# A gated attention and FFN block: the head laid anew, and the row statistics put between the low halves of the RELU

## The chip, the cores and the metric

One core of a Trainium2 chip runs the whole program. The metric is the device time in microseconds of one execution; the engines are PE (TensorE, matmul), DVE (VectorE), ACT (ScalarE), POOL (GpSimd) and SP (SyncE, which here only issues DMAs).

## What is computed

```python
# x: (8, 512, 256); all W of the attention 256x256; W1: (1024, 256), W2: (256, 1024)
xn = layernorm(x)                                  # no weight, no bias
q, k, v = (gelu(xn @ W1 + b1) @ W2 + b2 for each of q, k, v)     # gelu exact
scores = tril(q @ k.T) / sqrt(256 * 512)           # masked by zeros, no softmax
s = layernorm(scores @ v) * ln_w + ln_b
Wq = clip(round(W / (mean(abs(W)) + 1e-5)), -1, 1) # for W1 and W2 of the FFN
g = silu(relu(xn @ Wq1.T + b1) @ Wq2.T + b2)
out = x + s * g
```

## The kernel before

The kernel goes through the eight batches one after the other; each is a block of 512 rows of 256 channels. `batch(0, first=True)` is written out, batches 1 to 6 run in a hardware loop (on DVE and POOL batch 6 is written out), batch 7 is written out. Each engine has its own instruction stream in the order of the code, and semaphores (`wait_ge`, `then_inc`) join the streams. No scheduler moves anything.

To keep fp32 accuracy each operand is held as a high half (rounded, made by ACT or POOL) and a low half (source minus high half, made by DVE), and a product is three products: hi·hi, lo·hi and hi·lo (`split_product`, L771, whose inner matmul is L777). A batch goes, on PE, through these stages: layer one (six products of 512 columns, in PSUM banks 0 to 5, each followed by two GELUs on ACT and a low half `g_lo` on DVE), K (two products, banks 6 and 7), V (two banks), F1 (eight products against the quantised W1, each followed by two RELUs on ACT, L436 and L437, and a low half `r_lo` on DVE, L664), D and S (the scores), Y0 and Y1 (the FFN's second layer, which needs all eight `r_lo` and the quantised W2), O (scores times V) and Y2. A bank is claimed (`claim`, L748) by waiting for whoever reads its last content.

The statistics of x are made two batches ahead: `x_statistics(i + 2)`, L504, runs four `bn_stats` (L511) and `aggregate` (six small instructions, L490) on DVE, between `y_bias` and `o_scale(0)`. POOL takes the power for `x_rstd`, SP writes mean and rstd to DRAM and reads them back broadcast; POOL then normalises the transposed x.

Batch 0 has to do more. The *head* is what stands before it: DVE makes the statistics of x of batch 0 and normalises it in two halves (`x_normalise0`, L523), PE runs nine warm-up matmuls on constants (`WARM_UP`, L769) after POOL has made all five constants (`consts_made`, the last of them `causal`, L257), then `fold_biases` (six one-column products), then eight transposes of `xn` (L762), which ACT copies to `xT_hi` (L406) and DVE splits. Inside batch 0's layer one PE also folds W2q with W2k into one weight (`fold_weights`, FOLD in banks 6 and 7). The quantisation of W1 and W2 needs the sum of absolute values: of W1 by DVE (L613, after the second `g_lo`), of W2 by ACT (`abs_sum2`, after the last GELU); PE adds over partitions (`sum_partitions`, L799, into GAMMA in bank 3), DVE makes the threshold and compares (`quantise1` in two halves, `quantise2` for five eighths of W2), POOL compares the rest of W2 (`quantise_rest`, L300, after both halves of W1). `quantise2` stands behind all eight `r_lo` of batch 0, and PE's Y0 waits for it (`w2_quantized`, L883).

SP issues the loads in the order x(0) first half, W2q, W1k, W2k, W1q, x(1), W1v, W2v, W1 (raw1, 1 MB), W2 (raw2, 1 MB). ACT issues the other half of x(0), the bias columns, and later all four rows of `rows` broadcast to 128 partitions (L403, 512 KB).

## Time and profile before

| what | value |
|---|---|
| median of 3 runs | 320.83 us (319.23 to 322.04) |
| the profiled execution | 320.46 us |
| span of its trace | 318.7 us |
| PE busy | 307.7 us (97%) |
| DVE busy | 246.6 us (77%) |
| ACT busy | 220.1 us (69%) |
| POOL busy | 136.5 us (43%) |
| DMA | 19.06 MB, mean 60 GB/s |
| the chain that ended last | PE 49%, DVE 17%, ACT 15%, issue 15%, POOL 2% |

The span runs from the first to the last instruction on the core; the device time has 1.8 us more around it. Busy time of PE counts overlapping matmuls as one, so 97% says that PE nearly always had a matmul under way, and not that each ran at its best rate. The chain is read back from the last instruction to whatever released it. Line numbers are those of the kernel before.

### The profile page before, as it was taken

Reading aid. Unit: us, or ns where it says so; the run is one execution under the profiler, and the core shown is the slowest. Engines: PE = TensorE matmul, PEld = TensorE weight load, DVE = VectorE, ACT = ScalarE, POOL = GpSimd, SP = SyncE. Lnnn points to the kernel's source line nnn. Section 1 sums busy time; section 2 is a strip of 40 time slices with the busy share of each in tenths; the row PEclk is TensorE's granted clock in tenths of the full one; section 3 lists DMA queues with packets and bytes.
Section 4 is the critical chain, followed back from the end, with each engine's and each line's share of the span. In section 5 each row is a group of like instructions: output and inputs, shape, how many; then the busy total and the mean of one; then the engine's idle time right before and its main releaser. Section 6 shows DMA issues by size and latency. Waiting matters only on the chain.

```text
span 318.7 us, 5664 instructions
## 1 busy us (share of the span) xinstructions
PE 307.7 (97%) x1850; PEld 273.7 (86%) x1850; DVE 246.6 (77%) x544; ACT 220.1 (69%) x416; POOL 136.5 (43%) x105
## 2 busy tenths in 40 slices
PE   7899979999999999999999999999999999999994
PEld 7788879888997899888997889978998889988894
DVE  4589797965979669795879759796697958696687
ACT  3386936959487667858579494886678585794862
POOL 3691733349052570609334390526706093322200
PEclk9999999999999999999999999999999999999999
DMA  7950014520004100050003300041000500010001
GB/s 234 386 172 2 0 68 140 182 76 0 3 1 132 66 0 0 31 167 0 0 0 98 100 0 0 0 135 63 0 0 32 166 0 0 0 66 3 0 3 66
DMA packets 15212, 19.06 MB, mean 60 GB/s; under 512 B 1760, under 2 KB 12512, under 8 KB 15200
## 3 DMA queue, kind: packets, MB, share of 16 engines
q1 hardware_dynamic: 14496, 17.98, 17.1%
q10 hardware_dynamic: 704, 0.93, 0.8%
q8 instruction: 6, 0.10, 0.1%
q14 instruction: 6, 0.05, 0.1%
HBM read 14.69 MB, written 4.22 MB: 59 GB/s over the span
## 4 chain that ended last, share of the span: by engine, by line
PE 49%; DVE 17%; ACT 15%; issue 15%; POOL 2%; DVEq 1%; ACTq 0%; POOLq 0%
PE bank L777 47%; ACT r_hi L436 6%; ACT bank L437 5%; DVE gw L686 2%; DVE gw L701 2%; DVE e L675 2%; DVE x_stats L511 2%; DVE s L652 1%; PE bank L769 1%; DVE g_lo L593 1%; DVE s L649 1%; DVE e L608 1%; POOL o_rstd L343 1%; ACT s_hi L444 1%; DVE s_lo L659 1%
## 5 line engine op out<-in xcount | busy, mean ns | idle before, releaser
L664 DVE TENSOR_TENSOR r_lo<-bank,r_hi 128x512 fp32r<-128x512 f32 x64 | 44.1, 691 | 35.1 <-ACT bank L437 35.1
L436 ACT ACTIVATE r_hi<-bank,col 128x512 fp32r<-128x512 f32 x64 | 46.9, 733 | 24.5 <-PE bank L777 24.5
L437 ACT ACTIVATE bank<-bank,col 128x512 f32<-128x512 f32 x64 | 45.3, 709 | 0.0
L314 POOL TENSOR_TENSOR y<-y,xn 128x512 f32<-128x512 f32 x12 | 20.3, 1694 | 53.5 <-DMA xn<-x_norm_rows 53.5
L343 POOL TENSOR_TENSOR o_rstd<-o_var,neg_half 128x2 f32<-128x2 f32 x16 | 11.3, 704 | 68.5 <-ACT o_var L460 68.5
L777 PE MATMUL bank<-xT_lo,w1q 128*128 128x512 f32 x128 | 39.8, 392 | 0.0
L777 PE MATMUL bank<-xT_hi,w1q 128*128 128x512 f32 x128 | 39.8, 392 | 0.0
L444 ACT CAST s_hi<-s 128x512 fp32r<-128x512 f32 (+3 forms) x32 | 14.7, 461 | 32.7 <-DVE s L652 29.9
L417 ACT ACTIVATE g_hi<-bank,col 128x512 fp32r<-128x512 f32 x48 | 33.6, 699 | 5.1 <-PE bank L777 5.0
L777 PE MATMUL bank<-w2q,r_lo 128*128 128x256 f32 x256 | 35.0, 279 | 1.9 <-issue 1.9
L777 PE MATMUL bank<-w2q,r_hi 128*128 128x256 f32 x256 | 34.4, 277 | 0.0
L777 PEld LDWEIGHTS bank<-w2q,r_lo 128*128 128x128 f32 x256 | 31.7, 188 | 2.0 <-issue 2.0
L418 ACT ACTIVATE bank<-bank,col 128x512 f32<-128x512 f32 x48 | 32.2, 671 | 0.0
L777 PE MATMUL bank<-xT_hi,w_hi 128*128 128x512 f32 x96 | 31.2, 406 | 0.9 <-ACT xT_hi L406 0.9
L777 PEld LDWEIGHTS bank<-w2q,r_hi 128*128 128x128 f32 x256 | 31.4, 188 | 0.0
L593 DVE TENSOR_TENSOR g_lo<-bank,g_hi 128x512 fp32r<-128x512 f32 x48 | 30.4, 681 | 1.1 <-ACT bank L418 1.1
L777 PE MATMUL bank<-xT_lo,w_hi 128*128 128x512 f32 x96 | 30.7, 401 | 0.0
L777 PE MATMUL bank<-xT_hi,w_lo 128*128 128x512 f32 x96 | 30.7, 401 | 0.0
L349 POOL TENSOR_TENSOR gw<-gw,row 128x512 f32<-128x512 f32 x14 | 20.8, 1485 | 21.4 <-DVE gw L686 21.4
L777 PEld LDWEIGHTS bank<-xT_hi,w1q 128*128 128x128 f32 x128 | 24.0, 188 | 5.3
L777 PEld LDWEIGHTS bank<-xT_lo,w1q 128*128 128x128 f32 x128 | 23.4, 188 | 4.7 <-DVE neg_thr L543 0.2
L777 PEld LDWEIGHTS bank<-xT_lo,w_hi 128*128 128x128 f32 x96 | 18.4, 191 | 4.5
(131 smaller groups left out, 704.2 us busy)
## 6 DMA issues: line engine op xcount, KB each, us to landing
out<-x_all SPq DMA_DIRECT2D x15, 256.0 KB, 2.2
x_all<-in_x SPq DMA_DIRECT2D x7, 512.0 KB, 3.6
y<-in_x_t SPq DMA_DIRECT2D x6, 512.0 KB, 3.7
xn<-x_norm_rows SPq DMA_DIRECT2D x6, 512.0 KB, 3.5
x_all<-in_w1t SPq DMA_DIRECT2D x1, 1024.0 KB, 10.1
x_all<-in_w2t SPq DMA_DIRECT2D x1, 1024.0 KB, 12.2
row<-in_rows ACTq DMA_DIRECT2D x1, 512.0 KB, 8.0
x_all<-in_x SPq DMA_DIRECT2D x1, 256.0 KB, 3.2
```

The costliest lines, as they stand in the source:

```text
L314: nc.gpsimd.tensor_tensor(half, half, x_mean_all, ALU.subtract).then_inc(xT_centred, 1)
L343: nc.gpsimd.tensor_tensor(o_rstd[:, half], o_var[:, half], neg_half[:, half], ALU.pow).then_inc(o_rstd_made, 1)
L349: nc.gpsimd.tensor_tensor(gw[:, half], gw[:, half], row[:, ROW_LNB:ROW_LNB + 1].broadcast_to((P, 2, C)), ALU.add).then_inc(s_made, 1)
L417: nc.scalar.activation(g["hi"][:, m], pre[:], ACT.Gelu, bias=b1)
L418: nc.scalar.activation(pre[:], pre[:], ACT.Gelu, bias=b1).then_inc(l1_whole, 1)
L436: nc.scalar.activation(r["hi"][:, f], pre[:], ACT.Relu, bias=b1)
L437: nc.scalar.activation(pre[:], pre[:], ACT.Relu, bias=b1).then_inc(f1_whole, 1)
L444: nc.scalar.copy(s["hi"][:, at], s32[:, at]).then_inc(s_hi_made, 1)
L511: nc.vector.bn_stats(x_stats[:, t], x_all[:, b, t]).then_inc(x_stats_made, 1)
L593: nc.vector.tensor_tensor(g["lo"][:, m], bank[(AT_L1 + p) % BANKS][:], g["hi"][:, m].bitcast(FP32), ALU.subtract).then_inc(g_split, 1)
L664: nc.vector.tensor_tensor(r["lo"][:, f], bank[(AT_F1 + f) % BANKS][:], r["hi"][:, f].bitcast(FP32), ALU.subtract).then_inc(r_split, 1)
L777: last = nc.tensor.matmul(dst, a, b, start=(n == 0), stop=(n == len(pairs) - 1))
```

## The change

It has five parts.

1. **Start.** `ones` is made by DVE as its first instruction and no longer by POOL; the warm-up is 18 matmuls instead of 9, of ones by ones, and waits for `ones` alone. The transposes come ahead of `fold_biases`, which is cut in three: tiles 0 and 1, then one bias product, tiles 2 and 3, then the rest.
2. **Loads.** SP's order is new; the row `b2v` has a load of its own early on ACT's queue, the other three rows come last on SP's.
3. **Sum and quantisation of W1 and W2 in batch 0.** The absolute sum of W1 goes from DVE to ACT, behind the first GELU pair; the three `v_shifts` of ACT go ahead of the first GELU. PE adds W1's sum after the third product of layer one and W2's between the two V products (GAMMA moves to banks 6 and 5). DVE quantises the first half of W1 after the second `g_lo`, and the second half and W2 after the sixth, all ahead of `z_lo`, V and `r_lo`; the split of `e` goes behind V.
4. **POOL in batch 0.** W1v's split comes after two of W2v's centring steps; the normalising of x(1) goes in two pairs of tiles around `quantise_rest`.
5. **Statistics inside the loop.** In batches 1 to 5 the four `bn_stats` stand behind `r_lo` 0 to 3 and the six instructions of the aggregate behind `r_lo` 4. In batch 0 they stay where they were.

```diff
-WARM_UP = 9
+WARM_UP = 18
-        GAMMA = (bank[3][:, 0:1], bank[3][:, 1:2])
+        GAMMA = (bank[6][:, 2 * P + 1:2 * P + 2], bank[5][:, 0:1])
...
             sp.dma_start(x_all[:, 0, 0:2], x[0, 0:2 * P].rearrange("(t p) c -> p t c", p=P)).then_inc(x0_loaded[0], 16)
+            load_square(1)
             sp.dma_start(w2q_raw[:, :, 0:C], w_qkv[3].rearrange("(k p) c -> p k c", p=P)).then_inc(qkv_loaded[3], 16)
-            load_square(1)
+            load_square(0)
             load_square(4)
-            load_square(0)
             load_x(1)
-            load_square(2)
             load_square(5)
             sp.dma_start(raw1, w1t.rearrange("(k p) f -> p k f", p=P)).then_inc(raw1_loaded, 16)
+            load_square(2)
             sp.dma_start(raw2, w2t.rearrange("(f p) c -> p f c", p=P)).then_inc(raw2_loaded, 16)
+            sp.dma_start(row[:, ROW_F2:], rows[ROW_F2:].rearrange("(o r) c -> o r c", o=1).broadcast_to((P, 3, C))
+                         ).then_inc(rows_loaded, 16)
...
         def _(pool):
-            nc.gpsimd.memset(ones[:], 1.0).then_inc(consts_made, 1)
...
             def batch(i, first=False, second_last=False, last=False):
                 if first:
-                    pool.wait_ge(w1_quantized, 2)
+                    pool.wait_ge(x_rstd_made, 1)
+                    pool.wait_ge(xT_summed, CK)
+                    pool.wait_ge(w1_quantized, 1)
+                    xn1_tile(0)
+                    xn1_tile(1)
+                    pool.wait_ge(w2_quantized, 1)
                     quantise_rest()
-                    pool.wait_ge(w2_quantized, 1)
+                    xn1_tile(2)
+                    xn1_tile(3)
...
         def _(act):
+            def abs_sum1():
+                act.wait_ge(raw1_loaded, 16)
+                nc.scalar.activation(abs_out, raw1.rearrange("p a b -> p (a b)"), ACT.Abs,
+                                     accum_out=abs_sum[:, 0:1]).then_inc(abs1_summed, 1)
...
+            v_shifts()
...
                     if first and p < CK:
                         fold_hi(p)
-                    if first and p == 1:
-                        v_shifts()
+                    if first and p == 0:
+                        abs_sum1()
...
         def _(dve):
+            nc.vector.memset(ones[:], 1.0).then_inc(ones_made, 1)
...
                 g_lo(1)
                 if first:
-                    dve.wait_ge(raw1_loaded, 16)
-                    nc.vector.tensor_reduce(abs_sum[:, 0:1], raw1.rearrange("p a b -> p (a b)"), mybir.AxisListType.X,
-                                            ALU.add, apply_absolute_value=True).then_inc(abs1_summed, 1)
+                    thresholds(0)
+                    dve.wait_ge(thr_made, 2)
+                    quantise1(0)
                 g_lo(2)
...
                 g_lo(5)
-                dve.wait_ge(e_made, i + 1)
...
+                if first:
+                    dve.wait_ge(w1_quantized, 1)
+                    quantise1(1)
+                    dve.wait_ge(w1_quantized, 2)
+                    thresholds(1)
+                    quantise2()
+                    dve.wait_ge(w2_quantized, 1)
+                else:
+                    e_sum()
...
+                inside = not (first or second_last or last)
                 for f in range(FT):
                     r_lo(f)
-                if first:
-                    quantise2()
-                    dve.wait_ge(w2_quantized, 1)
+                    if inside and f == 0:
+                        dve.wait_ge(x_loaded, 16 * (i + 2))
+                        dve.wait_ge(x_norm_stored, 16 * i)
+                    if inside and f < TT:
+                        x_tile_statistics(i + 2, f)
+                    if inside and f == TT:
+                        x_moments(i + 2)
...
-                    if not second_last:
+                    if first:
                         x_statistics(i + 2)
...
         def _(pe):
-            pe.wait_ge(consts_made, 5)
+            pe.wait_ge(ones_made, 1)
             for _ in range(WARM_UP):
-                nc.tensor.matmul(bank[7][:, 0:P], ones[:], ident[:], start=True, stop=True)
+                nc.tensor.matmul(bank[7][:, 0:P], ones[:], ones[:], start=True, stop=True)
+            pe.wait_ge(consts_made, 4)
...
+                    if first and p == 2:
+                        pe.wait_ge(fold_read, CK)
+                        sum_partitions(0, abs1_summed)
...
-            fold_biases()
-            transpose_x(xn_made, AT_X0)
+            fold_z_bias(0)
+            transpose_x(xn_made, AT_X0, (2, 3))
+            fold_z_bias(1)
+            fold_d_bias()
```

**How the order moves on PE, ahead of batch 0.** Before, the first rows of PE's stream are the warm-up, the one-column products of the biases, the transposes of `xn`, and the first layer-one product.

```order
L769 MATMUL bank<-ident,ones 128x128 x9
L777 MATMUL bank<-col,w2q_raw 128x1 x4
L777 MATMUL bank<-col 128x1 x2
L762 MATMUL bank<-ident,xn 128x128 x8
L777 MATMUL bank<-xT_hi,w_hi 128x512 x2
```

After the change the same stretch of PE reads:

```order
L803 MATMUL bank<-ones 128x128 x18
L796 MATMUL bank<-ident,xn 128x128 x4
L812 MATMUL bank<-col,w2q_raw 128x1 x2
L796 MATMUL bank<-ident,xn 128x128 x4
L812 MATMUL bank<-col,w2q_raw 128x1 x2
L812 MATMUL bank<-col 128x1 x2
L812 MATMUL bank<-xT_hi,w_hi 128x512 x2
```

Nine matmuls came in at the front, and four of the six bias products now stand between the last transpose and the first layer-one product.

**How the order moves on DVE, in batch 0 behind the sixth g_lo.** Before, from `z_lo` on (the compare of W1's second half, V, the eight `r_lo`, then W2):

```order
L629 SCALAR_TENSOR_TENSOR z_lo<-bank,z_bias,z_hi 128x512 x2
L541 TENSOR_SCALAR thr<-bank 128x1
L543 TENSOR_SCALAR neg_thr<-bank 128x1
L548 TENSOR_SCALAR s<-x_all,neg_thr 128x1024
L550 SCALAR_TENSOR_TENSOR w1q<-x_all,thr,s 128x2x512
L640 TENSOR_TENSOR v<-bank,row 128x512 x2
L664 TENSOR_TENSOR r_lo<-bank,r_hi 128x512 x8
L548 TENSOR_SCALAR s<-x_all,neg_thr 128x1280
L550 SCALAR_TENSOR_TENSOR w2q<-x_all,thr,s 128x1280
L675 SCALAR_TENSOR_TENSOR e,d<-bank,d_const,ident 128x128 x4
```

After the change:

```order
L574 TENSOR_SCALAR s<-x_all,neg_thr 128x1024
L576 SCALAR_TENSOR_TENSOR w1q<-x_all,thr,s 128x2x512
L567 TENSOR_SCALAR thr<-bank 128x1
L569 TENSOR_SCALAR neg_thr<-bank 128x1
L574 TENSOR_SCALAR s<-x_all,neg_thr 128x1280
L576 SCALAR_TENSOR_TENSOR w2q<-x_all,thr,s 128x1280
L660 SCALAR_TENSOR_TENSOR z_lo<-bank,z_bias,z_hi 128x512 x2
L666 TENSOR_TENSOR v<-bank,row 128x512 x2
L622 CAST e_hi<-e 128x512
L624 TENSOR_TENSOR e_lo<-e,e_hi 128x512
L693 TENSOR_TENSOR r_lo<-bank,r_hi 128x512 x8
L709 SCALAR_TENSOR_TENSOR e,d<-bank,d_const,ident 128x128 x4
```

W2's compare moved from behind the eight `r_lo` to ahead of `z_lo`, and the split of `e` from ahead of it to behind V.

**How the order moves on DVE, in the loop's F1 stage.** After the change, from the fourth `r_lo` on (before, the eight `r_lo` follow each other with nothing but semaphore instructions between them):

```order
L693 TENSOR_TENSOR r_lo<-bank,r_hi 128x512
L525 ISA
L525 BN_STATS x_stats<-x_all 128x6
L692 REGISTER_ALU
L693 TENSOR_TENSOR r_lo<-bank,r_hi 128x512
L514 ISA
L515 TENSOR_TENSOR x_part<-x_stats 128x4
L516 TENSOR_TENSOR x_part<-x_stats 128x4
L517 SCALAR_TENSOR_TENSOR x_part<-x_stats 128x4
L518 REGISTER_ALU
L519 TENSOR_SCALAR x_norm<-x_part 128x4
L520 SCALAR_TENSOR_TENSOR x_part<-x_part 128x4
```

A `bn_stats` (and one more wait on a register) stands behind each of the first four `r_lo`, and the aggregate behind the fifth.

## Rows read from the trace of the kernel before

**Rows 1.** Waits of PE: engine, what, <- releaser: us in total, times, longest us.
```profile
PE bank L777 <- issue: 1.9, 1, 1.9
PE bank L777 <- DVE g_lo L593: 1.4, 5, 0.3
```

**Rows 2.** Windows of batches 1 and 2: stretch, length, busy us by engine, PEclk, DMA share, GB/s.
```profile
54.92:91.55 36.63, 36.63 (x227) 32.77 (x226) 29.66 (x65) 26.73 (x50) 15.04 (x10) 1.00 0.18 59
91.55:128.73 37.18, 36.88 (x227) 32.67 (x225) 29.14 (x64) 26.79 (x50) 16.74 (x12) 1.00 0.13 42
```

**Rows 3.** Timeline of PE, batch 0: start us, us, engine, line, what, [idle before <-releaser].
```profile
2.25 4.21 PE L769 MATMUL bank<-ident,ones 128*128 128x128 f32 x18 [2.25 <-POOL causal L257]
...
8.67 1.95 PE L762 MATMUL bank<-ident,xn 128*128 128x128 f32 x8
11.57 1.22 PE L777 MATMUL bank<-xT_hi,w_hi 128*128 128x512 f32 x2 [0.95 <-ACT xT_hi L406]
...
14.29 1.21 PE L777 MATMUL bank<-w2q_raw,raw_qkv 128*128 128x257 f32 x4
15.15 0.82 PE L777 MATMUL bank<-xT_hi,w_hi 128*128 128x512 f32 x2
...
16.74 1.03 PE L777 MATMUL bank<-w2q_raw,raw_qkv 128*128 128x257 f32 x4
...
43.03 1.17 PE L777 MATMUL bank<-w2q,r_lo 128*128 128x256 f32 x8 [1.91 <-issue]
...
52.16 1.03 PE L762 MATMUL bank<-ident,xn 128*128 128x128 f32 x8
```

**Rows 4.** Timeline of DVE, batch 0.
```profile
7.99 0.73 DVE L528 TENSOR_SCALAR xn<-x_all,x_norm 128x256 f32<-128x256 f32 x2 [0.27 <-POOL x_norm L269]
8.64 0.68 DVE L568 TENSOR_TENSOR w_lo<-raw_qkv,w_hi 128x512 fp32r<-128x512 f32 x1
...
12.39 1.40 DVE L511 BATCH_NORM_STATS2 x_stats<-x_all 128x6 f32<-128x256 f32 x4
...
26.62 0.75 DVE L548 TENSOR_SCALAR s<-x_all,neg_thr 128x1024 f32<-128x1024 f32 x1
27.41 1.28 DVE L550 SCALAR_TENSOR_TENSOR w1q<-x_all,thr,s 128x1024 fp32r<-128x1024 f32 x1
...
41.37 1.55 DVE L550 SCALAR_TENSOR_TENSOR w2q<-x_all,thr,s 128x1280 fp32r<-128x1280 f32 x1
```

**Rows 5.** Timeline of POOL, then of ACT, batch 0.
```profile
8.79 1.00 POOL L273 CAST w_hi<-raw_qkv 128x512 fp32r<-128x512 f32 x1 [0.84 <-DVE xn L528]
...
11.08 0.61 POOL L278 CAST w_hi<-raw_qkv 128x512 fp32r<-128x512 f32 x1
11.77 1.28 POOL L280 TENSOR_TENSOR w_lo<-raw_qkv,w_hi 128x512 fp32r<-128x512 f32 x1
...
24.59 1.92 ACT L384 ACTIVATE r_lo<-x_all 128x2048 fp32r<-128x2048 f32 x1
```

**Rows 6.** Window of 1 us; the DMA issue of W1 (KB, us from issue to landing).
```profile
18.00:19.00 1.00, 1.00 (x5) 0.78 (x5) 0.47 (x3) 1.00 (x5) 1.00 (x2) 1.00 0.39 124
...
x_all<-in_w1t SPq DMA_DIRECT2D x1, 1024.0 KB, 10.1
```

**Rows 7.** Timeline of DVE, then of POOL, in batch 2.
```profile
113.21 0.69 DVE L664 TENSOR_TENSOR r_lo<-bank,r_hi 128x512 fp32r<-128x512 f32 x1 [0.46 <-ACT bank L437]
...
125.33 1.40 DVE L511 BATCH_NORM_STATS2 x_stats<-x_all 128x6 f32 x4
...
127.46 0.87 DVE L686 SCALAR_TENSOR_TENSOR gw<-bank,o_rstd,row 128x256 f32<-128x256 f32 x2
...
130.40 0.88 DVE L686 SCALAR_TENSOR_TENSOR gw<-bank,o_rstd,row 128x256 f32<-128x256 f32 x2 [1.05 <-POOL o_rstd L343]
...
111.93 1.69 POOL L320 TENSOR_TENSOR y<-y,xn 128x512 f32<-128x512 f32 x1
...
128.40 1.30 POOL L349 TENSOR_TENSOR gw<-gw,row 128x512 f32<-128x512 f32 x1 [2.25 <-DVE gw L686]
```

More of the change, by code:

```diff
@@ L276, in _ @@
                                     ALU.subtract).then_inc(wq_split, 1)
+            pool.wait_ge(v_shift_made, CK + 1)
+            for k in range(CK):
+                nc.gpsimd.tensor_scalar(raw_qkv[:, 5, k], raw_qkv[:, 5, k], v_shift[:, k:k + 1], None,
+                                        ALU.add).then_inc(v_centred, 1)
+            x_rstd_of(1)
             pool.wait_ge(qkv_loaded[2], 16)
@@ L371, in _ @@
             act.dma_start(col[:], cols).then_inc(cols_loaded, 16)
-            act.wait_ge(consts_made, 5)
+            act.dma_start(row[:, ROW_B2V:ROW_F2], rows[ROW_B2V:ROW_F2].rearrange("(o r) c -> o r c", o=1).broadcast_to((P, 1, C))
+                          ).then_inc(b2v_loaded, 16)
+            act.wait_ge(consts_made, 4)
+            act.wait_ge(ones_made, 1)
             nc.scalar.activation(v_shift[:, 0:1], eps, ACT.Gelu).then_inc(gelu_loaded, 1)
@@ L389, in v_shifts @@
                 act.wait_ge(qkv_loaded[5], 16)
[L390 removed]
+                act.wait_ge(b2v_loaded, 16)
                 act.wait_ge(gelu_loaded, 1)
@@ L402, in _ @@
             weight_hi(1, 1)
-            act.dma_start(row[:], rows.rearrange("(o r) c -> o r c", o=1).broadcast_to((P, 4, C))).then_inc(rows_loaded, 16)
             for k in range(CK):
@@ L502, in aggregate, with x_tile_statistics, x_moments @@
                 nc.vector.scalar_tensor_tensor(var, part[:, 2], 1.0 / C, part[:, 3], ALU.mult, ALU.add).then_inc(made, 1)
+            def x_tile_statistics(b, t):
+                nc.vector.bn_stats(x_stats[:, t], x_all[:, b, t]).then_inc(x_stats_made, 1)
+            def x_moments(b):
+                aggregate(x_stats, x_part, x_mean, x_var, x_stats_made, STEPS * (b - 1) + TT, x_var_made)
             def x_statistics(b, second=False):
@@ L510, in x_statistics @@
                 for t in range(TT):
-                    nc.vector.bn_stats(x_stats[:, t], x_all[:, b, t]).then_inc(x_stats_made, 1)
-                aggregate(x_stats, x_part, x_mean, x_var, x_stats_made, STEPS * (b - 1) + TT, x_var_made)
+                    x_tile_statistics(b, t)
+                x_moments(b)
             def x_statistics0():
@@ L711, in batch @@
                     y_bias(AT_Y1, 2, 1, 3 * i + 2)
-                    if not second_last:
+                    if first:
                         x_statistics(i + 2)
@@ L755, in claim, with transpose_x @@
                 return bank[at % BANKS]
-            def transpose_x(made, at):
-                for t in range(TT):
+            def transpose_x(made, at, tiles=range(TT)):
+                for t in tiles:
                     pe.wait_ge(made, t + 1)
@@ L786, in fold_weights, with fold_z_bias, fold_d_bias @@
                                                     for k in range(CK)]).then_inc(folded, 1)
[L788 to L792 removed]
+            def fold_z_bias(n):
+                split_product(FOLD_Z[:, n:n + 1], [(w2qT[:, k, n * P:(n + 1) * P], b2k[:, k:k + 1])
+                                                   for k in range(CK)])
+            def fold_d_bias():
                 split_product(FOLD_D, [(b2q[:, k:k + 1].broadcast_to((P, P)), b2k[:, k:k + 1])
@@ L847, in batch @@
                     done.then_inc(v_summed, 1)
-                if first:
-                    pe.wait_ge(thr_made, 2)
-                    sum_partitions(1, abs2_summed)
+                    if first and n == 0:
+                        sum_partitions(1, abs2_summed)
                 for f in range(FT):
-                    if first and f == 1:
+                    if first and f == 3:
                         pe.wait_ge(thr_made, 4)
```

51 lines of the change are left out of this document (18 added, 33 removed).

## The prediction

> **What bounds the kernel now.** I read the waits of PE first, then the windows of one batch each, then the head in the timelines of all engines, then the DVE tail of one batch. PE is the bound, and its waits are few: one of 1.9 us, five of at most 0.3 us (1.4 us in all) for `g_lo` [rows 1], 2.25 us before its first matmul and 0.95 us before layer one of batch 0 [rows 3]. So time can be won in three places only: where PE waits, where its matmuls are slow, and ahead of the first useful one. The windows are laid from the first layer-one product of a batch to that of the next. Batch 1, without a wait for `g_lo`, takes 36.63 us with PE busy throughout; batch 2, with one, takes 37.18 with 36.88 busy [rows 2]. The idle 0.3 plus 0.25 for filling the array again make 0.55 us, five times.
>
> The head shows the second loss. The page's PEclk column grants 1.00 everywhere, so the level must be read from durations. The first layer-one product takes 2.72 us (11.57 to 14.29), the second, of the same six matmuls, 1.59 (15.15 to 16.74), and eight transposes take 1.95 us at 8.67 but 0.79 (52.16 to 52.95) at the end of batch 0 [rows 3]. The ratio of about two is that of the levels 1.2 and 2.4 GHz: PE ran at the lower one until nearly 15 us, though it had been at work, with one gap of 0.95 us, since 2.25. The third loss is the 1.91 us before Y0 at 43.03, where DVE's last W2 compare ends at 42.92 [rows 3, 4].
>
> **The loop.** What is late there is DVE. In batch 2 it makes the statistics of x at 125.33 (1.40 us), the aggregate runs to 127.46, and only then `o_scale(0)` [rows 7]. POOL's offset waits for that until 128.40 and takes 1.30; the second `o_rstd` is queued behind it, and DVE idles 1.05 us for it before `o_scale(1)` at 130.40 [rows 7]. Behind that stand the finish and the next batch's `g_lo`, for which PE's K stage waits. The edit takes 2.13 us (125.33 to 127.46) out of this chain. Not all of it reaches `g_lo`, since `o_scale(1)` also needs ACT's squares, but the chain has to come forward by only 0.3 us plus the refill, and the 1.05 us of idle time alone show more room than that. In the new place an `r_lo` of 0.69 us is followed by 0.46 idle [rows 7], eight times a batch. A `bn_stats` is 0.35, so four fit with 0.1 us to spare each; the aggregate of 0.73 overruns its slot by 0.27, which the next two slots, left empty, take back. So the last `r_lo`, for which Y0 waits, is not later. If it were, PE's Y0 would be. The cover is gone when a `bn_stats` with its register wait costs over 0.46 us, and the later slots absorb up to 1 us of that. The wait for `x_loaded` and `x_norm_stored` that comes with it is for things done long before the F1 stage. I price the loop at 5 x 0.55 = 2.7 us won; bounds: nothing (the wait moves to something else of the same length), and 2.75.
>
> In the new place POOL works beside it, in pieces such as 1.69 us at 111.93 [rows 7], where in the old one it was nearly idle. The head has the same meeting: `bn_stats` ran at 12.39 for 1.40 us while POOL's `w_lo` ran from 11.77 to 13.05 [rows 4, 5], no longer than with POOL idle. So no price for it; the opposite case is the slower rival below.
>
> **The start.** POOL's `causal`, the last constant, ends at 2.2 and PE starts at 2.25 [rows 3]. With `ones` as DVE's first instruction I estimate PE's start at 1.1. Nine warm-up matmuls took 4.21 us [rows 3], so 18 take 8.4 at the lower level and end at 9.5. At the upper level they take half. Before, the warm-up and the thin one-column products behind it left PE at the lower level; layer one raised it. A run of full matmuls twice as long should raise it on the way. The end of the warm-up is bounded by 9.5 (never raised) and 7.0 (5 of the 8.4 us at double rate); I take 8.2. `xn` is complete at 8.72 [rows 4]. Then: four transposes 0.4, the first bias product about 0.4, four transposes 0.4: the last ends near 9.5 (9.1 at best, by `xn`), where it was 10.62 [rows 3]. ACT's two copies and the handoffs put 0.95 us behind it [rows 3]; the four bias products left over lie beside them and may stick out by 0.3. Layer one starts at 10.8 instead of 11.57: 0.75 us won (bounds 1.4 won, 2.3 lost, the latter if the clock stays low all through: 9.5, then 2.7 us of transposes and bias products, and 1.6 of the rest). At the upper level from the first product on, layer one saves 2.72 - 1.59 = 1.1 us, and 0.1 on the fold product: 1.2.
>
> **Loads.** DMA is saturated to about 18.3 us (share 0.39 in the window 18 to 19) and moves the same bytes after, so what changes is who is last [rows 6]. W1 landed 10.1 us after issue, at 15.1, with four rows of `rows` going beside it [rows 6]. After, 640 KB less stand ahead of it; at 1 MB in roughly 2.7 us it lands near 13.5, W1v near 14.2, W2 near 17.3, the rows near 18.3. POOL's split of W1v takes about 2 us (0.6 and the 1.28 of [rows 5]), so it ends at 16.5 to 17.4, with what is queued before it; PE wants it for the fifth product, at about 18. I price it at nothing; its cover is a little under 1 us. Should W1v land at 16, PE waits 1 us there.
>
> **The sums on ACT.** The Abs of 2048 columns took 1.92 us, 2.0 with its read [rows 5]. The first GELU pair ends near 13.8, then the fold copy, then the Abs to about 16.3. PE asks for the sum behind its third product; three products at 1.5 to 1.6 and two fold products at 0.7 [rows 3] make 6.0 us, so at 16.8. Price nothing, cover 0.5. Behind the Abs on ACT are queued the other five GELU pairs, of some 1.2 us: they end at 22.7; before, the last ended at 24.6 [rows 5]. The sixth `g_lo` is DVE's affair: after the second at about 19.6 come the thresholds and W1's first compare (26.62 to 28.69, 2.1 [rows 4]), then four `g_lo`, spaced 0.6 like `r_lo` without gaps, so 24.3. V needs it; PE, with three more products and K's two at 1.4 each, is there at 16.8 + 7.2 = 24.0. Price: 0.3 us of a new wait (bounds 0 and 1).
>
> A row bears on this place: POOL's copy of 512 columns took 1.00 us at 8.79, while DVE's two-input `w_lo` ran from 8.64 to 9.32, and 0.61 at 11.08 [rows 4, 5]. So one engine can hold up the other by some 0.4 us. W1's first compare ran with POOL idle; at its new time POOL splits W1v and W2v in pieces of up to 1.28 [rows 5]. If DVE is the one held up, once for each of the two compares, V waits 1 to 2 us longer. I take nothing of it in the sum and give it a rival. The Trainium skill, SBUF — State Buffer, "Who interferes with whom", has this as a rule: VectorE and GpSimd share a port pair, held for a whole instruction by whoever comes first, and a VectorE operation with two SBUF inputs needs it against a GpSimd operation that reads SBUF. By that rule the compares do wait here, and the sum would be 315 to 316.
>
> **The compares ahead of r_lo.** After the sixth `g_lo` DVE does W1's second half (2.0), W2 (0.9 + 1.55, [rows 4]), two `z_lo` (1.3), two V reads (1.2), the split of `e` (1.1): it starts `r_lo` near 32.5 instead of 33.37, and with eight at 0.6 ends near 37.7. PE had 31.46 us from layer one to Y0 [rows 3]; less 1.91 and 1.2, plus 0.3, that is 28.65, so it reaches Y0 at 39.45. So Y0 finds W2 quantised, the last `r_lo` done, and POOL's rest of W2 done near 36. The 1.91 us before Y0 goes; next in line is that last `r_lo`, with 1.7 us to spare. Won: 1.9.
>
> **The sum.** Head and batch 0: 0.75 + 1.2 + 1.9 - 0.3 = 3.55. Loop: 2.7. Together 6.25. The profiled execution took 320.46 us (a span of 318.7 and 1.8 around it, which the change leaves alone), so 314.2; the median of the runs is 0.4 above that execution, which would give 314.6. I forecast 314.4.
>
> **The rivals.**
> - *The clock stays low through the warm-up.* For it: the warm-up of before left it low. Against: the new one is twice as long and runs up to the transposes. The head then gives nothing (layer one at 13.9, partly still at the lower level, 1.9 won back before Y0), the loop 2.7: about 318. Chance 0.12.
> - *The loop keeps its wait.* The chain behind the statistics goes on over POOL and ACT; if `o_scale(1)` were bound by ACT's squares at the same time, `g_lo` would be as late as now. Against: DVE's own 2.13 us lie in that chain. Time 317.0. Chance 0.10.
> - *A new wait in batch 0 ahead of V.* DVE's compares, held up by POOL, or W1v or the sum of W1 coming late, 1 to 2 us: about 316. For it the row of POOL's copy, against it that DVE was not seen to wait. Chance 0.17.
> - *Slower: the statistics under the low halves delay them.* If each `bn_stats` waits for a POOL piece of up to 1.7 us, four waits add up to 6.8 us a batch, the last `r_lo` comes late by what the slots (3.7 less 2.1) and PE's lead do not take, some 4 to 5 us, times five: 20 us, so 336. It decides, against the 3.55 of the head, once a `bn_stats` waits over about 0.7 us. The row in the head says that it doesn't. Chance 0.03.
> - My forecast, 313 to 315.8: chance 0.58.
>
> **Chances.** What a measurement here can tell from no change is about 1%, 3.2 us, so the border of faster is 317.6. Faster: 0.58 + 0.17 + 0.10 less what noise takes, some 0.84. Within 1%: 0.13. Slower: 0.03. The range of 312.8 to 317.6 leaves out most of the first rival and the slower one.
>
> **What would show it.** Right: 512-column pairs of the first layer-one product spaced 0.47 us from its start, which lies before 11.3; no idle PE before Y0 in batch 0; batches 2 to 6 at 36.6 us each and no wait of PE for `g_lo`; `bn_stats` at 0.35 between `r_lo` that still end as ACT lets them. Wrong: a layer-one product of 2.7 us; PE idle before the fourth or fifth product or before V; a batch over 37; a DVE row `r_lo` with a gap behind a `bn_stats`.

## The result and the profile after

The kernel after takes 323.49 us (median of 22 runs, 321.60 to 326.65) against 320.77 before (22 runs beside them, 319.23 to 323.65). The ratio is 1.009, 95% interval 1.0064 to 1.0116: slower by 0.9%, 2.7 us. One run of after, the one of 326.65 us, was in a slower state and is left out of the ratio. Forecast were 314.4 us and a range that ended at 317.6. The profiled execution took 323.19 us, its span 321.4.

The waits of PE in the kernel after (line, <- releaser: us in total, times, longest us):

```profile
PE bank L812 <- DVE r_lo L693: 5.8, 5, 1.4
PE bank L812 <- DVE g_lo L617: 1.2, 1, 1.2
PE bank L803 <- DVE ones L507: 1.1, 1, 1.1
PE bank L812 <- DMA w2q_raw<-in_W2q: 1.0, 1, 1.0
PE bank L812 <- ACT xT_hi L423: 0.3, 1, 0.3
```

Against [rows 1] the stall of 1.9 us before Y0 is gone and so are the five waits for `g_lo`. Five waits for `r_lo`, four times as long, have come in, one in each batch from 1 to 5, each ahead of Y0. The windows of batches 1 to 3 of the kernel after, each from its first layer-one product to the next batch's, columns as in [rows 2]:

```profile
52.99:91.40 38.41, 37.04 (x226) 33.05 (x225) 32.19 (x65) 26.74 (x50) 16.38 (x11) 1.00 0.13 42
91.40:129.32 37.92, 36.84 (x226) 32.83 (x225) 31.38 (x64) 26.80 (x50) 16.71 (x12) 1.00 0.13 42
129.32:167.07 37.75, 36.87 (x226) 32.86 (x225) 31.19 (x64) 26.79 (x50) 16.73 (x12) 1.00 0.12 42
```

They take 37.8 to 38.4 us where [rows 2] had 36.63 and 37.18. DVE is busy for 31.2 to 32.2 us, some 2 us more than in [rows 2], with as many instructions: something on it lasts longer. The timeline of PE shows how the head went:

```profile
1.12 6.61 PE L803 MATMUL bank<-ones 128*128 128x128 f32 x36 [1.12 <-DVE ones L507]
...
9.18 0.60 PE L812 MATMUL bank<-col,w2q_raw 128*128 128x1 f32 x4 [1.02 <-DMA w2q_raw<-in_W2q]
...
11.34 0.72 PE L812 MATMUL bank<-xT_hi,w_hi 128*128 128x512 f32 x2 [0.27 <-ACT xT_hi L423]
...
12.83 1.03 PE L812 MATMUL bank<-w2q_raw,raw_qkv 128*128 128x257 f32 x4
...
26.36 0.51 PE L812 MATMUL bank<-w_hi,g_hi 128*128 128x256 f32 x2 [1.24 <-DVE g_lo L617]
...
41.11 1.15 PE L812 MATMUL bank<-w2q,r_lo 128*128 128x256 f32 x8
```

Y0 of batch 0 starts at 41.11 instead of 43.03 [rows 3], and without a wait: the head gains 1.9 us, and batch 1 starts that much earlier too (52.99 for 54.92). From there to the end of the span the kernel before takes 263.8 us and the one after 268.4. So the head gave 1.9 and the loop took 4.6, which is the 2.7 us of the result. Two questions follow: what holds `r_lo` up, and why the head gave 1.9 and not 3.55.

For the first, the timeline of DVE in batch 2 of the kernel after, then POOL's for the same stretch:

```profile
112.00 0.42 DVE L525 BATCH_NORM_STATS2 x_stats<-x_all 128x6 f32 x1
112.55 0.69 DVE L693 TENSOR_TENSOR r_lo<-bank,r_hi 128x512 fp32r<-128x512 f32 x1
113.16 0.51 DVE L515 TENSOR_TENSOR x_part<-x_stats 128x4 f32<-128x4 f32 x1
...
113.85 2.30 DVE L519 TENSOR_SCALAR x_norm<-x_part 128x4 f32<-128x4 f32 x1
...
116.35 1.89 DVE L693 TENSOR_TENSOR r_lo<-bank,r_hi 128x512 fp32r<-128x512 f32 x3
```

```profile
111.71 1.93 POOL L342 TENSOR_TENSOR v_hi<-v,ones 128x1024 fp32r<-128x1024 f32 x1
113.72 2.40 POOL L345 TENSOR_TENSOR v_lo<-v,v_hi 128x1024 fp32r<-128x1024 f32 x1
```

The mean of the aggregate, a `tensor_scalar` of 128x4 elements, takes 2.30 us. It starts 0.13 us after POOL's `v_lo` and ends with it (116.15 and 116.12). The first addition (L515, two SBUF inputs) takes 0.51 and ends with `v_hi` (113.67 and 113.64); over the five batches it takes 0.32 to 0.80. The `bn_stats` beside them stay at 0.42. The same line before and after, all its instructions (ns min/median/max):

```profile
L499 DVE TENSOR_SCALAR x_norm<-x_part x9: 169/170/171, 5.2 to 238.6; 128x4 f32<-128x4 f32 x7, 128x2 f32<-128x2 f32 x2
```

```profile
L519 DVE TENSOR_SCALAR x_norm<-x_part x9: 170/2289/2302, 5.1 to 228.0; 128x4 f32<-128x4 f32 x7, 128x2 f32<-128x2 f32 x2
```

The five long ones are those of batches 1 to 5, with 2.29 or 2.30 us each. The Trainium skill, SBUF — State Buffer, "Who interferes with whom", has the rule: VectorE and GpSimd share a port pair, one of them holds it for a whole instruction, and what asks for it on VectorE, against a GpSimd operation that reads SBUF, is an operation with two SBUF inputs or one in a two-port mode (a `tensor_scalar` among them). A `bn_stats` reads one SBUF operand and does not ask. These rows of the loop agree in all three kinds.

Rows of batch 0 in the same trace do not. POOL's second compare for the rest of W2 has DVE's split of `e` beside it (DVE, then POOL):

```profile
33.74 0.91 DVE L622 CAST e_hi<-e 128x512 fp32r<-128x512 f32 x1
34.69 0.69 DVE L624 TENSOR_TENSOR e_lo<-e,e_hi 128x512 fp32r<-128x512 f32 x1
```

```profile
33.48 2.21 POOL L306 TENSOR_SCALAR w2q<-x_all,thr 128x768 fp32r<-128x768 f32 x1
```

By the rule `e_hi` would wait until 35.69. It takes 0.91 instead of the 0.42 that it has in all eight batches of the kernel before, so it is held up by 0.5 us only, and `e_lo`, with two SBUF inputs, runs in its usual 0.69 while POOL's instruction goes on, itself no longer than before (2.22). The eleven other traces with this order show the same. There the measurement decides: a wait until GpSimd's instruction ends is shown beside a `tensor_tensor` of POOL, and not beside this `tensor_scalar`. Why they differ is open.

What the rows of the loop don't show is whether the lock or the place beside `v_lo` is to blame for all of the 4.6 us. That is what the experiments ask first.

### The profile page after: what moved, and what is told of

Read it like the earlier page. It is cut to its first block, busy times and chain, and to the rows that moved or that the text cites. A ratio compares the mean times of both kernels' runs of the same rounds, so it can differ in the third digit from the quotient of the medians.

```text
span 321.4 us, 5700 instructions
## 1 busy us (share of the span) xinstructions
PE 307.4 (96%) x1868; PEld 274.4 (85%) x1868; DVE 257.4 (80%) x544; ACT 221.7 (69%) x418; POOL 136.2 (42%) x104
## 4 chain that ended last, share of the span: by engine, by line
PE 70%; issue 10%; ACT 8%; DVE 7%; DMA 3%; SPq 1%; POOL 0%; DVEq 0%
PE bank L812 70%; ACT bank L456 4%; DMA raw_qkv<-in_W2v 3%; ACT r_hi L455 2%; DVE r_lo L693 2%; DVE g_lo L617 1%; DVE x_part L515 1%; ACT r_lo L396 1%; DVE gw L720 1%; DVE s L574 0%; DVE gw L735 0%; SPq L193 0%; ACT o_square L411 0%; DVE w1q L576 0%; DVE x_all L737 0%
## 5 line engine op out<-in xcount | busy, mean ns | idle before, releaser
L693 DVE TENSOR_TENSOR r_lo<-bank,r_hi 128x512 fp32r<-128x512 f32 x64 | 42.8, 689 | 20.1 <-ACT bank L456 17.5
L463 ACT CAST s_hi<-s 128x512 fp32r<-128x512 f32 (+3 forms) x32 | 14.7, 461 | 38.2 <-DVE s L681 35.4
```

The lines of the kernel that those rows point to most:

```text
L463: nc.scalar.copy(s["hi"][:, at], s32[:, at]).then_inc(s_hi_made, 1)
L693: nc.vector.tensor_tensor(r["lo"][:, f], bank[(AT_F1 + f) % BANKS][:], r["hi"][:, f].bitcast(FP32), ALU.subtract).then_inc(r_split, 1)
```

## Experiments in the loop

Each theory was tried by taking one part back. All ratios are against the kernel before, run on the same chip; 95% intervals. The experiments ran in three groups, beside which the kernel before had medians of 320.84, 320.71 and 320.90 us, so the groups can be compared by their medians.

**The statistics back behind the loop's `y_bias`, all else as after.**

```diff
-                inside = not (first or second_last or last)
+                inside = False
...
-                    if first:
+                    if not second_last:
                         x_statistics(i + 2)
```

> The changed kernel with the statistics of x back behind y_bias in batches 1 to 5 (part 5 undone, parts 1 to 4 kept). Theory (the loss sits in part 5 alone: the mean's tensor_scalar waits up to 2.3 us for POOL's v_lo): no wait of PE for r_lo, batches 2 to 5 at 37.2 us as before, the tensor_scalar at 0.17 us everywhere, and the 1.9 us that the head gained are seen whole: about 319 against 320.8 of before. Rival (the head's new order costs something later, through batch 1 or the loads): 320.5 or more, with a new wait of PE in batch 0 or 1.

Measured: 319.04 us (318.58 to 319.33), ratio 0.9927 (0.9901 to 0.9953). So parts 1 to 4 alone win 1.8 us, and batch 2 is back at 37.22 with its wait for `g_lo`.

**The converse: part 5 alone, on the kernel before.**

```diff
+                inside = not (first or second_last or last)
                 for f in range(FT):
                     r_lo(f)
+                    if inside and f == 0:
+                        dve.wait_ge(x_loaded, 16 * (i + 2))
+                        dve.wait_ge(x_norm_stored, 16 * i)
+                    if inside and f < TT:
+                        x_tile_statistics(i + 2, f)
+                    if inside and f == TT:
+                        x_moments(i + 2)
...
-                    if not second_last:
+                    if first:
                         x_statistics(i + 2)
```

> The kernel before with part 5 alone. Theory: five batches of 37.9 to 38.3 us instead of 37.2, so 3.5 to 4.5 us slower than before, about 325, with the mean's tensor_scalar at 2.3 us. Rival (the meeting with v_lo comes only because the head shifted the phase of POOL against DVE): within 1 us of before.

Measured: 325.27 us (324.13 to 326.91), ratio 1.014 (1.009 to 1.0189). PE waits 6.0 us for `r_lo`, five times; the window of its batch 2:

```profile
91.58:129.73 38.15, 37.07 (x227) 33.06 (x226) 31.39 (x64) 26.80 (x50) 16.75 (x12) 1.00 0.12 41
```

Part 5 costs 4.4 us by itself, and 4.4 less 1.8 gives 2.6 of the 2.7 found. The two halves add up; the loss is wholly part 5's.

**Only the aggregate back, the four `bn_stats` left between the `r_lo`.**

```diff
-                    if inside and f == TT:
-                        x_moments(i + 2)
...
+                    if inside:
+                        x_moments(i + 2)
                     o_scale(0)
```

> The changed kernel with the four bn_stats left between the low halves, the six instructions of the aggregate back behind y_bias, where POOL is idle. Theory (only instructions with two SBUF inputs or a two-port mode wait for POOL, a bn_stats does not): r_lo as ACT lets them, no wait of PE for r_lo, batches 2 to 6 at 36.6 to 36.8, about 316.5. Rival (the bn_stats with their register waits already delay the low halves, or the chain behind keeps g_lo late): batches at 37.2 or more, 319 or more.

Measured: 316.92 us (315.92 to 317.53), ratio 0.9853 (0.9816 to 0.9889). PE waits neither for `r_lo` nor for `g_lo`. The windows of batches 1 and 2:

```profile
54.56:91.21 36.65, 36.65 (x226) 32.77 (x225) 29.73 (x65) 26.71 (x50) 16.32 (x11) 1.00 0.13 44
91.21:127.87 36.66, 36.66 (x227) 32.78 (x226) 29.15 (x64) 26.79 (x50) 16.77 (x12) 1.00 0.14 43
```

The `bn_stats` in the slots cost nothing, and 1.4 us less ahead of `o_scale(0)` is enough to end the wait for `g_lo`. What was wrong in part 5 is six instructions of 128x4, not the 128x256 ones that the slower rival named.

**Everything in its new place, but `v_lo` waits for the aggregate.** This tells contention from lateness: DVE's stream is that of after, and only POOL's start is moved.

```diff
                 pool.wait_ge(v_hi_made, i + 1)
+                if not (first or second_last or last):
+                    pool.wait_ge(x_var_made, i + 2)
                 nc.gpsimd.tensor_tensor(v["lo"][:], v32[:], v["hi"][:].bitcast(FP32),
```

> The changed kernel; in batches 1 to 5 POOL makes v_lo only after the aggregate is through (a wait on x_var_made ahead of it). All work of the change stays where it is; only the meeting goes. Theory: the mean's tensor_scalar falls from 2.3 to 0.17 us, v_lo starts some 0.4 us later, the first add of the aggregate still waits up to 0.8 us for v_hi, PE waits 0 to 0.3 us for r_lo: about 316.5 to 317.5. Rival (DVE's own load, or the register waits, delay r_lo): little moves, 321 or more.

Measured: 316.38 us (315.88 to 316.52), ratio 0.9843 (0.9809 to 0.9877); batches 1 and 2 at 36.63 and 36.65. Its DVE in batch 2, then POOL:

```profile
111.72 0.88 DVE L517 TENSOR_TENSOR x_part<-x_stats 128x4 f32<-128x4 f32 x1
...
112.78 0.17 DVE L521 TENSOR_SCALAR x_norm<-x_part 128x4 f32<-128x4 f32 x1
...
113.15 2.12 DVE L695 TENSOR_TENSOR r_lo<-bank,r_hi 128x512 fp32r<-128x512 f32 x3
```

```profile
110.67 1.90 POOL L342 TENSOR_TENSOR v_hi<-v,ones 128x1024 fp32r<-128x1024 f32 x1
113.29 2.41 POOL L347 TENSOR_TENSOR v_lo<-v,v_hi 128x1024 fp32r<-128x1024 f32 x1 [0.72 <-DVE x_var L524]
```

The mean takes 0.17 us again. The first addition still waits for `v_hi` (to 112.57), 0.7 us that the later slots absorb. One wait on POOL is worth 7.1 us against the kernel after.

**The mean in the form that also writes its accumulator.** By the Trainium skill, SBUF — State Buffer, "Who interferes with whom", that form does not ask for the port. If the rule holds, the mean runs at once, and the next instruction, a `scalar_tensor_tensor` with two SBUF inputs, waits in its place.

```diff
-                nc.vector.tensor_scalar(mean, part[:, 0], 0.5, None, ALU.mult).then_inc(steps, 1)
+                nc.vector.tensor_scalar(mean, part[:, 0], 0.5, 0.0, ALU.mult, ALU.add,
+                                        accum_out=small[:, 24:25]).then_inc(steps, 1)
```

> The changed kernel; the mean's tensor_scalar (x 0.5) in all batches also writes an accumulator. The page says that this form does not take the two-port mode, while instructions with two SBUF inputs still wait for a POOL operation that reads SBUF. Theory by that: the tensor_scalar takes 0.2 us in the loop instead of 2.3, and the scalar_tensor_tensor behind it, with two SBUF inputs, takes about 2 us instead: the aggregate ends where it did, time as the changed kernel, 323. Rival (only the two-port form waits): nothing waits, about 318. Second rival (any DVE instruction on small tiles waits, whatever its form): the tensor_scalar stays at 2.3.

Measured: 323.23 us (322.35 to 327.57), ratio 1.0076 (1.0046 to 1.0107), as slow as after. Its DVE in batch 2, then POOL:

```profile
112.99 0.16 DVE L519 TENSOR_SCALAR_CACHE_REDUCE x_norm<-x_part 128x4 f32<-128x4 f32 x1
...
113.08 2.21 DVE L521 SCALAR_TENSOR_TENSOR x_part<-x_part 128x4 f32<-128x4 f32 x1
```

```profile
112.86 2.41 POOL L345 TENSOR_TENSOR v_lo<-v,v_hi 128x1024 fp32r<-128x1024 f32 x1
```

The mean runs in 0.16 us in the middle of `v_lo`, the next instruction waits 2.21. Beside this `tensor_tensor` of POOL the wait belongs to the kind of operand access, not to the place or the size of the instruction.

## Experiments in the head

With the loop mended (the version in which `v_lo` waits, called the base below, 316.38 us), the head can be studied. Of its forecast 3.55 us after has 1.9. One caution goes with every Y0 below: five kernels (after, the base, and those with the statistics back, the aggregate back and the mean's accumulator) are the same up to there, and in their profiles Y0 starts at 41.11, 41.47, 41.77, 42.73 and 41.14. Two windows of the kernel after (4 to 8 us), with the DMA share and GB/s at the end:

```profile
4.00:6.00 2.00, 2.00 (x12) 2.00 (x11) 1.90 (x10) 0.73 (x3) 0.31 (x1) 1.00 0.64 185
6.00:8.00 2.00, 2.00 (x19) 1.92 (x18) 1.63 (x10) 0.07 (x1) 1.19 (x2) 1.00 0.82 218
```

The kernel before moves 305 and 329 GB/s there, the base 236 and 250. So the loads of W2 land later. The DMA issues of the kernel before, then of after (KB each, us from issue to landing):

```profile
w2q_raw<-in_W2q SPq DMA_DIRECT2D x1, 256.0 KB, 4.1
```

```profile
w2q_raw<-in_W2q SPq DMA_DIRECT2D x1, 256.0 KB, 7.3
...
row<-in_rows ACTq DMA_DIRECT2D x1, 128.0 KB, 7.0
```

Suspects: the early row `b2v` on ACT's queue, spread over 128 partitions, or SP's new order.

**`b2v` issued later on ACT's queue.**

```diff
-            act.dma_start(row[:, ROW_B2V:ROW_F2], rows[ROW_B2V:ROW_F2]...
             act.wait_ge(consts_made, 4)
...
             weight_hi(1, 1)
+            act.dma_start(row[:, ROW_B2V:ROW_F2], rows[ROW_B2V:ROW_F2]...
```

> Head study, on the kernel of e4 (median 316.4). The broadcast load of the row b2v is issued by ACT after the copy of W1k (where the four rows were loaded before the change) instead of in its first 2 us. Theory A (the early broadcast starves the loads beside it: DMA moved 180 to 236 GB/s from 4 to 8 us instead of 305 to 329): W2q lands by 6.5 us after the start instead of 9.1 to 9.7, PE does not wait for it, layer one starts 0.7 to 1 us earlier, about 315.3. Theory B (SP's order is what makes W2q late): W2q still lands after 8.5, no gain.

**SP's order of before, `b2v` early.**

```diff
-            load_square(1)
             sp.dma_start(w2q_raw[:, :, 0:C], ...
-            load_square(0)
+            load_square(1)
             load_square(4)
+            load_square(0)
             load_x(1)
+            load_square(2)
             load_square(5)
             sp.dma_start(raw1, ...
-            load_square(2)
```

> Head study, on the kernel of e4. SP's loads in the order of the kernel before (the three other rows still last), b2v early as in the change. Theory A (the broadcast starves them): W2q, now first in the order, lands near 6.5 since it is issued 0.5 us earlier, but DMA still dips at 4 to 8 us and the squares behind it come late. Theory B (SP's order is the cause): the dip is gone and everything lands as before the change. Time 315.5 to 316.5 in both; the DMA windows decide.

The windows of 4 to 8 us, with `b2v` late, then with the old order:

```profile
4.00:6.00 2.00, 2.00 (x12) 2.00 (x11) 1.28 (x7) 0.00 (x0) 0.00 (x0) 1.00 1.09 349
6.00:8.00 2.00, 2.00 (x15) 1.82 (x14) 1.86 (x11) 0.71 (x2) 0.97 (x2) 1.00 1.09 352
```

```profile
4.00:6.00 2.00, 2.00 (x18) 2.00 (x17) 1.90 (x10) 0.28 (x2) 0.34 (x1) 1.00 0.86 220
6.00:8.00 2.00, 1.58 (x15) 1.36 (x14) 1.63 (x10) 0.00 (x0) 1.16 (x2) 1.00 0.98 198
```

It is the early row, not the order. In both orders the load issued ahead of it (W1k, or W2q in the old order, at 1.3 us) lands within 4.1 us and the next one takes 7.3 and 7.7. Late, it lets W2q land after 4.8 us, PE doesn't wait for it, and layer one starts at 10.86. But the time is 316.09 (315.49 to 316.18), only 0.3 below the base, and the intervals of their ratios overlap: ACT's three `v_shifts` now wait until 13.03 for `b2v`, the first GELU stands behind them, PE waits 0.7 us for the sum of W1 and 1.2 for the sixth `g_lo`, and Y0 starts at 41.25 (41.47 in the base). One late row was exchanged for another. The old order costs: 317.53 (317.23 to 318.12), Y0 at 42.32, since W1k lands after 7.7 us and PE waits 1.3 for `xT_hi`. (The granted clock was at 0.50 for a time in its profile, as in the base's.)

**All bias products behind the eight transposes.**

```diff
-            transpose_x(xn_made, AT_X0, (0, 1))
+            transpose_x(xn_made, AT_X0)
...
             fold_z_bias(0)
-            transpose_x(xn_made, AT_X0, (2, 3))
             fold_z_bias(1)
```

> Head study, on the kernel of e4. All eight transposes stand ahead of the first bias product, so that none of them waits for W2q. Theory (PE's wait of 1.0 to 1.7 us for W2q delays the transposes behind it, and its idle time and thin products let the clock fall): the last transpose ends near 8.9 instead of 10.3 to 10.8, but the six bias products then wait for W2q at 9.1 to 9.7 and the first layer-one product stands behind them in PE's order: it starts only 0.3 to 0.5 us earlier. About 316.

Measured: 316.55 us (315.25 to 316.98). Layer one starts at 10.37 and Y0 at 40.43, 1.0 us before the base's, but the median does not show it: its runs spread over 1.7 us, and only the lowest, which is the profiled one, is 1 us below the base. What it does show is the clock. Windows of 12 to 14 us, of the base, then of this kernel (PEclk is the third number from the end):

```profile
12.00:14.00 2.00, 2.00 (x6) 1.61 (x5) 1.97 (x9) 0.80 (x4) 0.27 (x1) 0.50 1.05 378
```

```profile
12.00:14.00 2.00, 2.00 (x11) 1.65 (x10) 1.53 (x9) 1.84 (x8) 0.42 (x1) 1.00 1.03 380
```

In the base PE waits 1.2 us for W2q at 8.2 to 9.5 and then runs one-column products between its transposes; the granted clock falls to 0.50, 1.2 GHz, and a layer-one product takes 2.5 us (11.62 to 14.13). The profiles with the aggregate back, with the mean's accumulator, with the old order and with part 5 alone show such a fall too. That of after doesn't (1.00 all along, first product 1.49 us), nor does that with the statistics back, though its wait for W2q was 1.3 us. So it comes in some executions of the same head.

What the fall costs is not settled. The profile with the accumulator has it and reaches Y0 at 41.14, after at 41.11: PE, a microsecond later, no longer waits for the sixth `g_lo`. With the aggregate back it lasted until 18 us, and Y0 came at 42.73. Of the 21 runs of after in its ratio, nine with a mean granted clock of at least 0.998 have a median of 322.55 us and the twelve below it 323.88; the base's four show no such difference (316.31 and 316.52 at 0.991, 316.45 and 315.88 at 0.999 and 1.000).

**The warm-up of before, nine matmuls.**

```diff
-WARM_UP = 18
+WARM_UP = 9
```

> Head study, on the kernel of e4, with 9 warm-up matmuls instead of 18. Theory C (the longer warm-up raises the clock, but the wait for W2q and the one-column products behind it let it fall again in some executions, as the granted 0.50 between 11 and 18 us in two profiles shows): with 9 the transposes run at the lower level or the upper one, layer one starts at the lower level more often; 0.5 to 1.5 us slower than e4. Rival (the length of the warm-up does not matter, since layer one's level is decided behind it): the same as e4 within 0.5 us.

Measured: 317.61 us (317.44 to 318.67). The timeline of PE:

```profile
1.12 4.21 PE L805 MATMUL bank<-ones 128*128 128x128 f32 x18 [1.12 <-DVE ones L509]
7.59 1.09 PE L798 MATMUL bank<-ident,xn 128*128 128x128 f32 x4 [2.27 <-DVE xn L556]
...
12.95 1.20 PE L814 MATMUL bank<-xT_hi,w_hi 128*128 128x512 f32 x2
```

Four transposes take 1.09 us (0.60 in after) and layer one starts at 12.95 with matmuls at the lower level. The longer warm-up is worth 1.2 us against the base; the runs lie apart, though the intervals of the two ratios (0.9871 to 0.9948 here) just touch.

**`b2v` late and the bias products behind, together** (the two edits above).

> On the kernel of e4: b2v loaded late (h1) and the bias products behind all transposes (h3). Theory: no wait for W2q, layer one starts near 10.3 us, but ACT's v_shifts, ahead of the first GELU, then wait for b2v until about 13 as in h1, so the GELUs, the sum of W1, the first compare and the sixth g_lo stay where they are and V waits 1.2 us or more: Y0 near 41, about 316, no better than h3 alone. Rival (the start of layer one decides): 315.3.

Measured: 315.58 us (315.35 to 315.91), Y0 at 40.89. PE waits 1.1 us for the sum of W1 and 1.2 for `g_lo`: `v_shifts` is now first on the path. As its theory had it, the time is no better than that of the biases behind alone (315.25 to 316.98).

**Bias products behind, and POOL's split of W2v waits for W1's first compare.**

```diff
             pool.wait_ge(w2v_hi_made, 1)
+            pool.wait_ge(w1_quantized, 1)
             nc.gpsimd.tensor_tensor(w["lo"][:, 4], raw_qkv[:, 5], w["hi"][:, 4].bitcast(FP32),
```

> On the kernel of e4 with the bias products behind the transposes (h3); POOL's w_lo of W2v (1.29 us, two inputs) starts only when the first half of W1 is quantised. Theory (the first compare took 1.48 us instead of 0.75 because it waited for that w_lo): the compare takes 0.75 us, the sixth g_lo comes 0.7 us earlier, PE's wait ahead of V falls from 1.2 to about 0.5, 0.5 us faster than h3. Rival (the wait for g_lo has another cause, or V then waits for w2v_split instead): the wait stays at 1.2.

Measured: 315.56 us (315.28 to 316.14), Y0 at 40.38. The compare, in the kernel after, then here:

```profile
21.11 1.48 DVE L574 TENSOR_SCALAR s<-x_all,neg_thr 128x1024 f32<-128x1024 f32 x1
```

```profile
21.07 0.75 DVE L577 TENSOR_SCALAR s<-x_all,neg_thr 128x1024 f32<-128x1024 f32 x1
```

In after, POOL's `w_lo` runs from 20.75 to 22.04 beside it. Without that the compare takes its 0.75 us, and the wait for `g_lo` falls from 1.2 to 0.5. The 0.7 us do not reach Y0, which was at 40.43 with the biases behind alone: in this execution W2v landed later, the first GELU started at 14.06 instead of 13.38, and PE waited 0.9 us for the sum of W1 instead of 0.4. So the cause of the long compare is shown, a gain in time from this edit alone is not.

**All of it, and the shift of `b2v` taken out of `v_shifts`**, to stand behind the first fold copy on ACT:

```diff
-                act.wait_ge(b2v_loaded, 16)
                 act.wait_ge(gelu_loaded, 1)
-                for k, src in enumerate([raw_qkv[:, 5, 0], raw_qkv[:, 5, 1], row[:, ROW_B2V]]):
+                for k, src in enumerate([raw_qkv[:, 5, 0], raw_qkv[:, 5, 1]]):
...
                     if first and p == 0:
+                        row_shift()
                         abs_sum1()
```

`row_shift` is the third pass of that loop, with its wait for `b2v`; POOL waits for it only ahead of the row's own centring. Both are left out of the cut.

> On the kernel of e4, all of it together: b2v late, bias products behind the transposes, POOL's w_lo of W2v behind the first compare, and the shift of the b2v row behind the first fold copy, so that the first GELU waits for W2v alone. Theory: ACT's first GELU starts near 12 us instead of 14, the sum of W1 is there when PE asks, PE waits under 0.5 us in all between layer one and Y0, Y0 near 39.5 instead of 41.1: about 314.5. Rival (DVE in batch 0 is the bound): Y0 near 41, 316.

Measured: 313.42 us (313.28 to 313.65), ratio 0.976 (0.9718 to 0.9801). The waits of PE, and Y0 in its timeline:

```profile
PE bank L812 <- DVE ones L516: 1.1, 1, 1.1
PE bank L821 <- DVE g_lo L626: 0.2, 1, 0.2
```

```profile
38.79 1.15 PE L821 MATMUL bank<-w2q,r_lo 128*128 128x256 f32 x8
```

Y0 is 2.7 us earlier than in the base, the time 3.0 less, and the runs lie within 0.4 us. This version beats both kernels: 2.4% below before, 3.1% below after. No run took the shift alone, so what it gives without the other three edits is not shown.

## Why the prediction was wrong, point by point

- **The loop, 2.7 us won: it lost 4.6.** The reasoning on where the wait for `g_lo` comes from held: with the meeting removed, batches take 36.65 us, no `g_lo` is late, and the 2.7 us are there. The step that failed is "the aggregate of 0.73 overruns its slot by 0.27, which the next two slots, left empty, take back", and under it "so no price for it". The prediction asked of `bn_stats` alone whether POOL's work beside it would hold it up, took the answer from one row of the head, and let it stand for the six instructions behind. These ran beside 4.3 us of POOL work with two inputs (`v_hi`, `v_lo`). Priced by the rows: 2.1 us more on the mean, 0.2 to 0.6 on the first addition; the slots and PE's lead take some of it, the last `r_lo` is late by 0.9 to 1.4 us, and refilling PE comes to that.
- **The slower rival** (chance 0.03) had the right mechanism, DVE waiting for a piece of POOL's, but on the wrong instruction. It set the point of decision at 0.7 us for each of four `bn_stats`; a single wait of 2.1 us decides as well. The prediction cited the very rule, for the compares of batch 0, and did not run it over the other operations that the change moved beside POOL. This was the costliest omission. (By its own terms the rival's time is 337 us, not 336.)
- **"DVE was not seen to wait"** is a wrong reading of the trace of before. In batch 2 of that kernel, DVE, then POOL:

```profile
132.02 1.56 DVE L703 TENSOR_TENSOR x_all<-x_all,gw 128x512 f32 x1
```

```profile
131.35 1.68 POOL L349 TENSOR_TENSOR gw<-gw,row 128x512 f32<-128x512 f32 x1 [0.99 <-DVE gw L686]
```

  This addition has two SBUF inputs. In each of batches 0 to 6 its first half starts while POOL's multiply runs and takes 1.56 to 1.67 us; the second half takes 0.69. The price of the meeting stood in every batch before the change.
- **The new wait ahead of V, 0.3 us (rival: 1 to 2): 1.2 us.** The first compare took 1.48 instead of 0.75, by the mechanism that the rival named (POOL's split of W2v); the second met only the last 0.3 us of POOL's `tensor_scalar` for x(1) and took 0.88.
- **Start of layer one, 10.8: 11.34.** The warm-up ended at 7.6 and not 8.2, since the clock rose within it, and the first product took 1.49 us, as forecast. Then PE waited 1.0 us for W2q. The step that failed is "moves the same bytes after, so what changes is who is last": bytes and order were counted, the rate was taken as given, and it fell by a third and more over 4 us. W1, W1v, W2 and the rows landed at 15.5, 16.2, 19.2 and 20.1 us, forecast 13.5, 14.2, 17.3 and 18.3. With `b2v` late they land at 13.2, 13.9, 16.9 and 17.9: the count was right, the rate was the fault.
- **The sum on ACT, cover 0.5.** The same dip made W2v land late, `v_shifts` waited 1.6 us for it and the first GELU started at 14.10. The prediction put the three `v_shifts` on the path to the first GELU and did not ask what they wait for. Layer one being late as well, PE hardly waited for the sum here; once the head was faster (`b2v` late, biases behind) it waited 1.1.
- **The 1.9 us before Y0** went, as forecast, and nothing took their place.
- **The clock**: right for the profiled execution, but the forecast asked only when it rises, not whether it stays up behind the wait and the one-column products.

With the loop as priced and the head as measured the time is that of the base, 316.4, inside the range. With the four edits of the head as well it is 313.4, 1.0 below the forecast; those edits were not part of the change, so that this lies close to 314.4 does not confirm the forecast.

## What to carry to other kernels

When instructions move to another place, list for each of them, the smallest first, what GpSimd runs beside the new place and whether both ask for the shared port: beside a `tensor_tensor` of GpSimd the price of a 0.17 us instruction is the rest of GpSimd's instruction. Look in the trace at hand for an instruction of the kind that is already held up. A wait put on the long GpSimd operation, where that has room, is a cheaper cure than moving the short one back. Ahead of the first useful product, check each early load for the rate of the others beside it, and each instruction ahead of the first activation for what it waits for.

## What the runs showed of the hardware

- A VectorE `tensor_scalar` of 128x4 (0.17 us) took 2.29 to 2.30 us beside a GpSimd `tensor_tensor` of 2.40, five times out of five. In the form that writes an accumulator it took 0.16 in the middle of such an operation. `bn_stats` stayed at 0.42 beside `v_hi`. Beside a GpSimd `tensor_scalar` of 2.21 us a VectorE cast took 0.91 instead of 0.42 and a two-input `tensor_tensor` its usual 0.69.
- A row of 1 KB spread over 128 partitions (128 KB on ACT's queue), issued among the first loads, brought the total from 305 and 329 GB/s down to 185 and 218 for 4 us. Issued later it took as long (6.9 us), W2q landed after 4.8 us, and the total stayed at 352 to 391 from 6 to 12 us. Why it slows the others was not settled: in after the engines' share of busy time fell with the rate (0.64 and 0.82), but with SP's old order it was 0.86 and 0.98 at 220 and 198 GB/s.
- Behind waits of PE and one-column products ahead of layer one the granted clock fell to 0.50 in some executions, until 14.7 to 18 us, and not in others of the same head, with waits for W2q of 1.2 to 1.7 us where it fell and of 1.0 and 1.3 where it didn't. With `b2v` late, the products still between the transposes and no wait for W2q, it stayed at 1.00, and so it did in the four profiles with the bias products behind the transposes. Each is one profile, and what brings the clock down is open: of the eight runs of the two kernels with the biases behind and `b2v` early, three have a mean granted clock of 0.991 to 0.993, as low as the base's profile with the fall (0.991).
